# Last two attention pairs scaled in rows of dimensions, tail by query halves, loads moved up

## The reference

```python
q = (M @ Wq.T).reshape(e, h, dh).transpose(1, 0, 2)
kv = x @ Wkv.T + bkv
sim = jnp.where(mask, jnp.einsum('hid,hjd->hij', q, k) * dh ** (-0.5), -1e9)
out = jnp.einsum('hij,hjd->hid', softmax(sim), v)          # then heads side by side
m = layer_norm(out @ Wo.T + bo + M)
ffn = jax.nn.relu(m @ W1.T + b1) @ W2.T + b2
z = layer_norm(ffn + m)
```

## Time and profile before

| | us |
|---|---|
| three runs | 683.79 (median), 680.31, 1226.24 |
| the profiled execution: time, span | 684.72, 682.9 |
| PE busy in it | 632.4 (93%) |
| DVE busy | 549.7 (80%) |
| ACT, POOL busy | 363.8, 254.8 |
| chain that ended last: PE, DVE | 59%, 16% |

### The profile page before, as it was taken

How to read it: one execution, slowest core, us unless ns; L and a number is a source line. 1 busy time by engine, 2 the same in 40 slices (tenths; PEclk the granted TensorE clock), 3 DMA queues, 4 the chain that set the end, 5 groups by cost and what they waited for, 6 DMA issues and landing times.

```text
span 682.9 us, 10600 instructions
## 1 busy us (share of the span) xinstructions
PE 632.4 (93%) x3382; PEld 396.0 (58%) x3382; DVE 549.7 (80%) x685; ACT 363.8 (53%) x659; POOL 254.8 (37%) x312
## 2 busy tenths in 40 slices
PE   4999999999999999999999999999998697999996
PEld 3675555545665555655555566555653344688884
DVE  3889999999998999899999999899998836334334
ACT  5576565565565566556565565556564313333332
POOL 3561632264224632163226522363212404422224
PEclk9999999999999999999999999999999898799999
DMA  8078989878988889888997888888777982032221
GB/s 285 9 201 210 221 215 254 206 201 211 230 222 206 216 215 252 192 206 209 233 230 196 212 223 227 204 218 207 198 194 187 257 231 72 31 93 93 92 91 61
DMA packets 56098, 128.29 MB, mean 188 GB/s; under 512 B 15856, under 2 KB 20976, under 8 KB 55792
## 3 DMA queue, kind: packets, MB, share of 16 engines
q1 hardware_dynamic: 45296, 101.97, 58.2%
q10 hardware_dynamic: 10752, 25.70, 14.1%
HBM read 23.80 MB, written 1.05 MB: 36 GB/s over the span
## 4 chain that ended last, share of the span: by engine, by line
PE 59%; DVE 16%; issue 7%; SPq 5%; ACT 4%; POOL 3%; DMA 3%; ACTq 2%; DVEq 0%; POOLq 0%
PE tail L943 16%; PE slot L889 13%; DVE st L744 7%; PE tail L815 7%; PE slot L1001 7%; PE slot L996 7%; PE slot L815 6%; SPq L387 4%; DVE prob L734 4%; ACT prob L579 2%; PE tail L952 2%; ACTq L631 2%; DVE acc L751 2%; DMA wq_raw<-in_wq 1%; PE slot L847 1%
## 5 line engine op out<-in xcount | busy, mean ns | idle before, releaser
L579 ACT ACTIVATE prob<-prob,negmax 128x896 f32<-128x896 f32 x224 | 233.6, 1043 | 203.9 <-DVE negmax L734 201.4
L734 DVE CUSTOM_DVE_ANT_0 prob<-slot,lower,negmax_old 128x896 f32<-128x896 f32 x224 | 248.9, 1149 | 36.1 <-PE slot L889 25.4
L744 DVE STREAM_TRANSPOSE st<-prob 128x1792 f32<-128x1792 f32 x112 | 228.5, 2040 | 4.9 <-DMA pt<-st 4.7
L943 PE MATMUL tail<-pt,val 128*64 128x512 f32 x784 | 184.5, 607 | 8.1 <-ACT outT_sb L610 5.9
L943 PEld LDWEIGHTS tail<-pt,val 128*64 128x64 f32 x784 | 51.4, 138 | 102.9 <-issue 94.4
L889 PE MATMUL slot<-k_hi,q_hi 64*128 64x448 f32 x448 | 94.8, 414 | 10.9 <-DVE negmax L734 6.8
L889 PEld LDWEIGHTS slot<-k_hi,q_hi 64*128 64x128 f32 x448 | 43.3, 183 | 78.7 <-issue 71.2
L889 PE MATMUL slot<-k_hi,q_lo 64*128 64x448 f32 x448 | 84.0, 363 | 0.0
L889 PE MATMUL slot<-k_lo,q_hi 64*128 64x448 f32 x448 | 83.7, 362 | 0.0
L467 POOL TENSOR_TENSOR total<-total,alpha 128x8 f32<-128x8 f32 x28 | 5.8, 206 | 189.6 <-ACT alpha L635 189.5
L489 POOL TENSOR_TENSOR k_lo<-k_raw,k_hi 128x896 fp32r<-128x896 f32 x27 | 57.1, 2115 | 3.9 <-POOL k_hi L486 0.2
(11 more groups left out here) (127 smaller groups left out, 844.6 us busy)
## 6 DMA issues: line engine op xcount, KB each, us to landing
pt<-st SPq DMA_DIRECT2D x672, 112.0 KB, 3.0
pt<-st ACTq DMA_DIRECT2D x224, 112.0 KB, 3.4
w_raw<-in_w SPq DMA_DIRECT2D x32, 256.0 KB, 2.9
x_raw<-in_x SPq DMA_DIRECT2D x13, 448.0 KB, 4.3
mask_raw<-in_mask SPq DMA_DIRECT2D x7, 448.0 KB, 4.5
mt_raw<-in_mt SPq DMA_DIRECT2D x2, 512.0 KB, 7.8
wo_raw<-in_wo SPq DMA_DIRECT2D x1, 1024.0 KB, 6.9
m_res<-in_mn SPq DMA_DIRECT2D x1, 1024.0 KB, 5.1
```

The costliest lines, as they stand in the source:

```text
L579: nc.scalar.activation(unit, unit, ACT.Exp, bias=negmax[:, p, u:u + 1], scale=-1.0, accum_out=psumrow[:, p, u:u + 1]).then_inc(exp_done, 1)
L734: nc.vector.tensor_tensor_reduce(out=prob[:, i % 2, h].rearrange("p (b n) -> p b n", b=2), in0=slot[:, j, :, :HALF], in1=lower[:, i].rearr ...
L744: nc.vector.transpose(st[:, g].rearrange("p b k (t i) -> p k b t i", t=2)[:, :, :, t2], prob[:, i % 2].rearrange("p h (k b i) -> p (h k) b ...
L943: last = nc.tensor.matmul(outT[DH * h:DH * h + DH], val[:, val_at(i, parity ^ (p < 0)), head(p, h)], moving, start=(i == 0), stop=(i == KT ...
```

## The change

The loads of m_res, bo and b2 go to the end of pair 1 of the last chunk, that of wo ahead of the first moves of pair 2; POOL's work on them follows pair 3's second and third tile. The buffers of the tail are laid out anew for this, and `val_at` swaps which three slots of `val` even chunks use. In the tail, pairs 2 and 3 are no longer brought back to queries in rows: P multiplies `acc` by the identity into the output bank, PV adds to it there, v spreads the reciprocals over 64 rows per head by a product with the identity, ACT copies them to `invT_sb`, and d scales, adds the bias and splits. Pair 2 takes all its PV ahead of the last transposition; pair 3's PV (w), projection, norm (l, s, m) and the first two up products (u) go by halves of 256 queries. The second group of moves of pair 3 is shared eight and eight by SP and ACT. The diff, cut to its core:

```diff
     ('S E0 E1 W0 W1 W2 W3 X M1',
      'S E0 V3 E1 Z K H L X B1',
      'S E0 E1 F W4 W5 W6 C A X M0',
-     'S E0 E1 V4 X B0'),
+     'S E0 E1 V4 X B0 I0'),
     ('S E0 V5 E1 W0 W1 X M1',
      'S E0 V6 E1 Z K H J0 L X B1',
-     'S E0 E1 F W2 W3 W4 A X R1 M0',
-     'S E0 E1 W5 W6 C X B0 J1 I'),
+     'S E0 E1 F W2 W3 W4 A X R1 I1 M0',
+     'S E0 E1 W5 W6 C X B0 J1'),
     ('S E0 E1 W0 W1 W2 W3 X M1',
-     'S E0 E1 Z F K H L A X B1',
-     'S E0 E1 W4 W5 W6 C X M0',
-     'S E0 E1 N0 X B0 O'),
+     'S E0 E1 Z F K H L A X B1 O0',
+     'S E0 E1 W4 W5 W6 C X M0 O1',
+     'S E0 E1 N0 X B0'),
...
         a, b = PAIRS - 2, PAIRS - 1
-        out.extend([("F", 1, 0), ("A", 1, 0), ("N", 1, 0)])
-        out.extend([("X", b, 3), ("M", b, 1), ("B", b, 1), ("Z", b, 0), ("I", b, 1), ("O", b, 1)])
-        out.extend([("G", 0, 0), ("T", 0, 0), ("D", 0, 0)])
-        out.extend([*(("W", a, kt) for kt in range(3)), ("G", 1, 0), ("T", 1, 0), ("D", 1, 0)])
-        out.extend([*(("W", a, kt) for kt in range(3, KT)), ("C", a, 0), ("Y", 0, 0), ("F", a, 0), ("A", a, 0), ("N", a, 0)])
-        out.extend([("Y", 0, 1), ("Y", 0, 2), ("Y", 0, 3), ("G", a, 0), ("T", a, 0), ("D", a, 0)])
-        out.extend([*(("W", b, kt) for kt in range(KT)), ("C", b, 0), ("Y", 1, 0), ("F", b, 0), ("A", b, 0), ("N", b, 0)])
-        out.extend([("Y", 1, 1), ("Y", 1, 2), ("Y", 1, 3), ("G", b, 0), ("T", b, 0), ("D", b, 0)])
-        out.extend([("Y", 2, t) for t in range(QT)])
+        first, second = (("W", a, kt) for kt in range(KT)), (("X", b, 3), ("M", b, 1), ("B", b, 1), ("Z", b, 0), ("I", b, 2))
+        out.extend([("F", 1, 0), ("A", 1, 0), ("N", 1, 0), ("i", a, 0), ("P", a, (0, 1)), *first, *second])
+        out.extend([("G", 0, 0), ("T", 0, 0), ("G", 1, 0), ("T", 1, 0), ("v", a, 0), ("D", 0, 0), ("D", 1, 0), ("d", a, (0, 1))])
+        out.extend([("Y", 0, 0), ("Y", 0, 1), ("i", b, 0), ("v", b, 0), ("P", b, (0,)), ("w", b, 0), ("d", b, (0,))])
+        out.extend([("Y", 1, 0), ("Y", 1, 1), ("c", 0, 0), ("c", 1, 0), ("c", 2, 0), ("Y", 2, 0), ("Y", 2, 1), ("P", b, (1,)), ("w", b, 1)])
+        out.extend([("l", 0, 0), ("s", 0, 0), ("l", 1, 0), ("e", 0, 0), ("d", b, (1,)), ("s", 1, 0), ("m", 0, 0)])
+        out.extend([("Y", 0, 2), ("Y", 0, 3), ("m", 1, 0), ("e", 1, 0), ("Y", 1, 2), ("Y", 1, 3), ("Y", 2, 2), ("Y", 2, 3), ("e", 2, 0)])
+        out.extend([("u", 0, 0), ("u", 1, 0), ("l", 2, 0), ("s", 2, 0), ("l", 3, 0), ("s", 3, 0), ("r", 0, 0), ("r", 1, 0)])
+        out.extend([("m", 2, 0), ("m", 3, 0), ("u", 0, 1), ("u", 1, 1), ("r", 2, 0), ("r", 3, 0)])
...
+        wo_raw = late("wo_raw", [P, PAIRS, DM], F32)
...
+        up_to("x_raw")
+        m_res = late("m_res", [P, QT, DM], F32)
+        bo_sb = late("bo_sb", [P, DM], F32)
+        b2_sb = late("b2_sb", [P, DM], F32)
...
-            return KT + kt if kt < TWICE and parity else kt
+            return kt if kt < TWICE and parity else TWICE + kt
...
+        def turns(c, p, i):
+
+            return ((0, 1), (2, 3)) if c == CHUNKS - 1 and p == PAIRS - 1 and i == 1 else ((0, 1, 2), (3,))
...
-            bank = (slot[:, 2, 1], tail[:, 0], tail[:, 1])[t % 3]
+            bank = (outT, slot[:, 2, 1], tp, outT)[t]
...
+        def out_bank(p):
+
+            return outT if p == PAIRS - 2 else tp
+
+        def halves_of(parts):
+            return slice(parts[0] * E // 2, (parts[-1] + 1) * E // 2)
+
+        def by_quadrant(t, order):
+            return t.rearrange(f"p ({order}) -> p a t i", a=QUAD, t=2, i=LANES)
...
-                        for turn in (0, 1, 2):
+                        for turn in turns(c, p, i)[0]:
...
                     if kind == "I" and i == 0:
-                        sp.wait_ge(filled[KEYS_RING], keys_use(pair_no(c, PAIRS - 1)) + 1)
-                        sp.wait_ge(v_filled, KT * CHUNKS)
+                        sp.wait_ge(xlo_ready, 2 * CHUNKS)
                         sp.wait_ge(lower_ready, CHUNKS * QT)
-                        sp.wait_ge(klo_done, PAIRS * CHUNKS - 1)
-                        sp.dma_start(wo_raw[:], wo).then_inc(wo_in, 16)
-                    if kind == "I" and i == 1:
+                        sp.wait_ge(pv_done, KT * PAIRS * (CHUNKS - 1))
                         sp.dma_start(m_res[:], mn).then_inc(mres_in, 16)
-                        sp.wait_ge(pv_done, KT * PAIRS * (CHUNKS - 1))
                         sp.dma_start(bo_sb[:], bo.to_broadcast([P, DM])).then_inc(bias_in, 16)
                         sp.dma_start(b2_sb[:], b2.to_broadcast([P, DM])).then_inc(bias_in, 16)
+                    if kind == "I" and i == 1:
+                        sp.wait_ge(filled[KEYS_RING], keys_use(pair_no(c, PAIRS - 1)) + 1)
+                        sp.dma_start(wo_raw[:], wo).then_inc(wo_in, 16)
+                    if kind == "I" and i == 2:
+                        sp.wait_ge(v_filled, KT * CHUNKS)
+                        sp.wait_ge(klo_done, PAIRS * CHUNKS - 1)
                         for j in range(2):
                             sp.dma_start(w1_raw[:, j], w1[j]).then_inc(w1_in[j], 16)
...
                     if kind == "O" and i == 0:
                         pool.wait_ge(wo_in, 16)
+                        pool.wait_ge(v_filled, KT * CHUNKS)
...
+                    if kind == "l":
+                        inv_deviation(p, 0)
+                    if kind == "r":
+                        pool.wait_ge(m_ready, p + 1)
+                        nc.gpsimd.tensor_tensor(m_res[:, p], norm[:, p], b2_sb[:], ALU.add).then_inc(mres2, 1)
...
-                        for turn in (3,):
+                        for turn in turns(c, p, i)[1]:
...
+                    if kind == "v":
+                        act.wait_ge(invT_filled, p - PAIRS + 3)
+                        nc.scalar.copy(invT_sb[:, p % 2], gather_bank(p)).then_inc(invT_copied, 1)
+                    if kind == "d":
+                        cols, made = halves_of(i), p + i[0] + 1
+                        act.wait_ge(half_scaled, made - 1)
+                        nc.scalar.activation(ao2[0][:, p, cols], outT_sb[:, cols], ACT.Identity, bias=bv_sb[:, p:p + 1]).then_inc(aohi, 1)
+                    if kind == "c" and p < 2:
+                        up_weights_hi(p, p)
+                    if kind == "c" and p == 2:
+                        down_weights_hi(0, 0)
+                    if kind == "s":
+                        layer_scale(p, 0, m_ready)
+                    if kind == "m":
+                        act.wait_ge(mT_filled, p + 1)
+                        nc.scalar.copy(mT2[0][:, :, P * p:P * p + P], m_bank(p)).then_inc(mThi, 1)
...
+                    if kind == "i":
+                        dve.wait_ge(stats_kept, 2 * (n + 1))
+                        nc.vector.reciprocal(inv[:, p], total[:, p]).then_inc(inv_ready, 1)
+                    if kind == "d":
+                        cols, made = halves_of(i), p + i[0] + 1
+                        dve.wait_ge(invT_copied, p - PAIRS + 3)
+                        if p == PAIRS - 2:
+                            dve.wait_ge(pv_done, KT * (n + 1))
+                        else:
+                            dve.wait_ge(half_done, i[0] + 1)
+                        if made > 3:
+                            dve.wait_ge(aolo, made - 1)
+                        for g in i:
+                            own = halves_of((g,))
+                            nc.vector.tensor_tensor(by_quadrant(outT_sb[:, own], "t a i"), by_quadrant(out_bank(p)[:, own], "a t i"),
+                                                    by_quadrant(invT_sb[:, p % 2, own], "t a i"), ALU.mult).then_inc(half_scaled, 1)
+                        dve.wait_ge(half_scaled, made - 1)
+                        dve.wait_ge(aohi, made)
+                        nc.vector.scalar_tensor_tensor(out=ao2[1][:, p, cols], in0=outT_sb[:, cols], scalar=bv_sb[:, p:p + 1],
+                                                       in1=ao2[0][:, p, cols], op0=ALU.add, op1=ALU.subtract).then_inc(aolo, 1)
+                    if kind == "l":
+                        if p == 0:
+                            dve.wait_ge(mres_ready, 1)
+                            dve.wait_ge(xposed, QT * PAIRS * CHUNKS)
+                        dve.wait_ge(proj_done, p + 1)
+                        layer_norm(p, slot[:, p // 2, p % 2], 2 * p)
+                    if kind == "e" and p < 2:
+                        up_weights_lo(p, p)
+                    if kind == "e" and p == 2:
+                        down_weights_lo(0, 0)
+                    if kind == "m":
+                        dve.wait_ge(mThi, p + 1)
+                        nc.vector.tensor_tensor(mT2[1][:, :, P * p:P * p + P], m_bank(p), mT2[0][:, :, P * p:P * p + P],
+                                                ALU.subtract).then_inc(mTlo, 1)
...
-                                                    start=(i == 0), stop=(i == KT - 1))
+                                                    start=(i == 0 and not (final and p == PAIRS - 2)), stop=(i == KT - 1))
```

(115 more changed lines are left out.)

65 lines of the change are left out of this document (10 added, 55 removed).

## The result

The changed kernel takes 685.9 us in the median of 16 runs, the kernel before 683.95 in the median of 16: ratio 1.0036, interval 1.0023 to 1.005 (the ratio leaves out the one execution of 1226.24 us). It is slower by 2.0 us in the medians and by some 2.4 us by the ratio, where I had forecast 1 us less. The first down product of the profiled execution starts at 594.59, 2.24 later than before; of that, 0.25 is there at 481 already.

The account below looks back on a forecast made before the run. With the PE-busy feed-forward loop unchanged, the chain of waits up to the first down product decided: -1.65 + 5.4 - 0.55 - 4.25 = -1.05 us, giving 682.8 us, range 677.5 to 686.7.

Parts of the forecast that it names:

- The early loads: Loads of m_res, bo, b2 and wo moved earlier: 2.62 MB taking 6.7 us, against 4.8 us free from 506 to 520.
- The backlog of 1.9 us: DMA work from the early loads expected to remain when pair 2's moves begin, where before 2.7 us of wo came halfway.
- rival A: Early loads choke the moves; pair 2's first group lands late, tile 0's transposition waits 3 to 4 us; +3.1, 685.9; chance 0.13.
- The scaling beside POOL: Pair 1's scaling on DVE ends with or just behind POOL's operation on m_res and wo, costing at most 1 us.
- ACT's issues: Behind the last transposition, ACT issues eight moves in 5.4 us before T0 and D0, with v behind them.
- B: Rival: full queues hold back ACT's eight issues, sixteen moves taking 7.3 us; T0 starts 1.9 later, 684.7; chance 0.12.
- v and P: PE's added products: v 0.21 us per matmul, 1.7 for eight or 3.4 at half clock; P 0.21 each.
- C: Rival, faster: v and P cost what transposes cost, 0.11 us each; about -2.3, so 680.5; chance 0.20.
- The clock: PE falls to half clock after its idle time from about 546, and again after 582 for the up half.
- D: Rival, faster: the clock stays full over the gaps at 546 and 582; 678.7; chance 0.05.
- E: Rival: the wait at 542 stays, pair 2's second group being bound by DMA share, not wo; about -0.3, 684.1; chance 0.10.
- the term of -1.65: Last transposition ends at 546.3 instead of 547.95, since DVE's wait for a move at tile 2 shrinks.

Follow-up runs that it names:

- a1: Changed kernel with m_res, bo and b2 loaded behind pair 2's second moves and POOL's sum behind the last pair's statistics; 681.93 us, ratio 0.9988 to the kernel before.
- c2: Changed kernel with POOL's sum of m_res and bo behind the last pair's statistics, its load unmoved; 686.06 us, one run.
- b2: Kernel before with wo loaded ahead of pair 2's moves and all sixteen moves of the last group on SP; 683.35 us, ratio 1.0008.
- a7: Changed kernel with the last group's moves again twelve on SP and four on ACT; 681.91 us, ratio 0.9978 to the kernel before.
- a2: Changed kernel with all sixteen moves of the last group issued by SP, none by ACT; 678.42 us, ratio 0.9938 to the kernel before.
- a3: Changed kernel with the edits of a1 and a2 together; 673.79 us, ratio 0.987 to the kernel before.
- a4: a3 with the first feed-forward weights loaded right behind m_res, ahead of the last pair's moves; 677.21 us, ratio 0.9903 to the kernel before.
- a5: Changed kernel with a1's and a7's edits, ACT's four moves behind its part of d(a), pair 3's reciprocal earlier; 672.95 us, ratio 0.9852 to the kernel before.
- b1: Kernel before with only the load of wo moved ahead of pair 2's first group of moves; 681.75 us, ratio 0.9978.
- c1: Changed kernel with the first two up products whole behind the last transpose instead of first halves ahead; 686.2 us, ratio 1.0053 to the kernel before.

## Why the prediction was wrong, by its own steps

| us | forecast | measured |
|---|---|---|
| last transposition ends, against before | -1.65 | +1.0 |
| from there to the first projection | 10.6 | 10.3 |
| first projection to the end of the last | 22.2 | 22.5 |
| from there to the first down product | 12.2 | 12.8 |
| first down product | 591.3 | 594.59 |

**The early loads are the step that failed.** The backlog of 1.9 us was too small, and I charged it to pair 2's second group alone. I priced only the group that comes last and passed over the first one: M(1,1) stands directly behind I0, and both DVE's transposition of pair 2's tile 2 and PV of pair 1 want it. In 506 to 520 the engines moved 254 GB/s for 14 us, 1.3 MB more than before, so that about half of the 2.6 MB, in loads or in moves held up by them, was still to come at 520. The free time of 4.8 us that I summed over this stretch lies in the wrong place; in the kernel before, most of it comes behind 516, when nearly all of M(1,1) has left SP:

```profile
516.00:518.00 2.00, 2.00 (x16) 1.28 (x16) 1.94 (x1) 0.55 (x2) 0.36 (x1) 1.00 0.54 120
...
518.00:520.00 2.00, 2.00 (x12) 0.74 (x10) 1.93 (x3) 0.74 (x1) 0.00 (x0) 1.00 0.00 0
```

Up to 516 only 1.8 us are free (share 0.82 over 10 us). By that my own 6.7 us of loads leave 4.9, an estimate; the group, which before had landed by 518, landed at 523.2, at least 5.2 later. DVE's wait for it is 2.7 us. PE was idle for 2.1 us (1.0 before) and then needed 5.35 for 16 records instead of 3.65, which is the half clock. These two run side by side and don't add: each leaves its engine some 3 us late at the next scores. That is rival A's mechanism one group earlier than I put it, with nearly its price: forecast 3.1, while a1, which undoes it, gains 3.3 together with the 0.84 of the next point. I gave A 0.13 though the window row from 520 on, which I named for it, already stood at 0.96.

**The scaling beside POOL** was named and bounded at 1 us: 0.84 (c2). The row at 590.96 was the right one, and b2's 3.35 shows how far the same wait can go. The rule on the shared ports in the Trainium skill (SBUF — State Buffer, "Who interferes with whom") agrees with both: each time the scaling ends 0.55 us behind POOL's operation, as if it had had to wait for all of it.

**ACT's issues** I priced right (5.4, measured 5.67) and judged wrongly only in that I left them in the sum without asking what they give: nothing. Undoing the even split gains 4.0 us (a7, 3.0 of it the edit's own in the profile), taking all issues off ACT 6.7 (a2), since the clock comes along. B, queues holding ACT up for 7.3 us, did not occur. The sentence of the Trainium skill (DMA: Bandwidth & Descriptors, "Issuing engines are not separate DMA queues") that a second issuing engine saves only issue time fits a2: sixteen issues by SP alone cost the end nothing. The issue time itself is not always hidden: in b2, whose PV wants the group sooner, PE waits 3.12 us for it.

**v and P.** The upper bound was right: 16 records for eight products, 1.58 at full clock (forecast 1.7) and 2.85 at half (3.4). C falls. P took 1.06 for four (0.85) and 0.71 for two (0.43). **The clock** went to half after the pause at 549, as forecast, and again at 588. The second time varies between kernels with the same instructions there: in a1, a2, a3 and a7 it falls as in the changed kernel, in a4 and c2 on the down products just behind, and in a5 on neither (1.67 against 2.91). What decides was not tried. D falls for the kernel as changed.

**E** didn't occur as such: the wait at 542 is gone.

**The loop** was taken as untouched, 84.35 us; it takes 83.46. That gives back 0.9 of the 2.2 in the profiled executions, more on this below.

So the forecast missed by 3.3 us at the first down product: 2.65 in the first row of the table, 0.6 in the last. Of the 2.65, 2.1 are there when tile 2's transposition starts (542.57 against 540.5): the wait that I wanted to remove is gone, and the choked moves of pair 1 had already cost 3. The other 0.6 lie behind it and are POOL's 0.84, part of which the forecast had in. So the term of -1.65 failed, and those behind the last transposition held within 0.6.

The form itself looks like a gain, of a size that is less sure: from the first projection to the first down product it takes 35.3 us instead of 39.2, and a5 33.2. But v of pair 2 stands ahead of that stretch in the new form. From the end of the last transposition, with four issues on ACT in each, a7 takes 42.5 us, the kernel before 44.4 and b1 43.3, one execution each. What of that is due to the dimensions in rows and what to the halves stays open but for the 1.2 us of c1.

## What to carry to other kernels

A load that is moved up must be priced at the group of moves that stands directly behind it in its queue, and at who waits for that group, before any group further on; free DMA time summed over a stretch says too little. DMA issues on a compute engine belong behind the work that others wait for: in the new form the same sixteen moves cost 0 or 6.7 us by which engine issued them and when. The engine that takes them over needs the time, though: in the old form, which wants them sooner, PE waited 3.1 us (b2). Where the TensorE idles before a stage and its rows show the half clock behind such a pause, a wait ahead of the stage costs its own length and the half clock behind it: 2.1 us of idle PE brought it at 523, 1.0 us in a7 did not. Two profiles should be compared over a stretch with a common start, not by the starts alone: here they differed by up to 5 us before anything that had been changed.

## What the runs showed of the hardware that was not expected

In the feed-forward loop, whose instructions are the same, 12 matmuls of 512 columns take 2.80 us in the three kernels with the old tail (before, b1, b2) and about 2.77 in those with the new one. The straight-line down products at the end take 8.53 for 36 in both. Buffers lie elsewhere and the program has other lengths ahead of the loop; which of these does it wasn't tried. It is worth 0.9 us, and a change that moves buffers can't be judged closer than that by its own steps.

The plain f32 products of v, 64 output rows and 128 columns, take 0.20 us for each of the eight. PV's need 6.23 for 14 of 512 columns, 0.445 each, and those by halves 3.2 for 14 of 256, 0.23 each, about half as much per column in both. PV's alternate between the two halves of the array, and v has four of one half and then four of the other; that this order is the cause, and not the shortness of the products, is not shown.
